# Gate rows for a mixture-of-experts product: from a matrix product on TensorE to DMA reads of a scratch in DRAM

## The reference, cut to what matters

```
xt = layernorm(x)                                  # 1024 tokens x 128
gates = sigmoid(xt @ expert_sel.T)                 # 1024 x 32 experts
gate_full = only the four largest gates of a token kept, the others 0
scores = relu(einsum('nd,edf->nef', xt, keys))     # 32 experts, 64 values each
scores = scores * gate_full[:, :, None]
out = einsum('nef,efv->nv', scores, values)
x = x + tanh(g_ffn) * out
```

## Time and profile before

| | |
|---|---|
| median of 3 runs | 144.35 us (143.78 to 144.61) |
| the profiled execution | 143.71 us |
| its span, first to last instruction | 141.9 us |
| mean granted TensorE clock | 0.984 of full speed |
| PE busy | 130.3 us (92%) |
| DVE busy | 105.3 us (74%) |
| ACT busy | 72.2 us (51%) |
| POOL busy | 9.0 us (6%) |
| DMA packets | 2170, 4.27 MB |

### The profile page before, as it was taken

The page is one execution under the profiler, slowest core; times in us unless marked ns, Lnnn a source line. Parts: engine busy times, 40 slices in busy tenths (PEclk is TensorE's granted clock), DMA queues, the critical chain, the costliest instruction groups (busy, mean ns, idle before and its releaser), DMA issues.

```text
span 141.9 us, 2125 instructions
## 1 busy us (share of the span) xinstructions
PE 130.3 (92%) x672; PEld 86.3 (61%) x672; DVE 105.3 (74%) x338; ACT 72.2 (51%) x172; POOL 9.0 (6%) x27
## 2 busy tenths in 40 slices
PE   5999696998889997999899999999999999999990
PEld 5958393585445864878556346366545666676860
DVE  1799969597989785986989643945694689769852
ACT  5368675587682763336234451331214666866620
POOL 7970000000000000000000000000000000000000
PEclk9999999599999999999999999999999999999998
DMA  4697000000000000000000000000000000000004
GB/s 92 206 387 330 9 5 0 2 0 0 0 5 0 0 0 2 5 0 0 0 0 0 5 0 0 0 2 0 0 0 0 0 0 0 7 0 0 0 0 148
DMA packets 2170, 4.27 MB, mean 30 GB/s; under 512 B 240, under 2 KB 1648, under 8 KB 1904
## 3 DMA queue, kind: packets, MB, share of 16 engines
q1 hardware_dynamic: 2160, 4.15, 8.5%
HBM read 3.63 MB, written 0.52 MB: 29 GB/s over the span
## 4 chain that ended last, share of the span: by engine, by line
PE 77%; DMA 7%; DVE 5%; issue 3%; SPq 3%; ACT 2%; DVEq 0%; ACTq 0%
PE bank L907 11%; PE bank L727 11%; PE bank L831 9%; PE bank L729 9%; PE bank L728 8%; PE bank L897 7%; DMA values<-values_in 7%; PE bank L762 3%; PE bank L841 3%; PE bank L785 2%; PE bank L758 2%; PE bank L736 2%; PE bank L772 2%; PE bank L814 2%; PE bank L816 1%
## 5 line engine op out<-in xcount | busy, mean ns | idle before, releaser
L541 DVE SCALAR_TENSOR_TENSOR keys<-bank,inT 128x512 f32<-128x512 f32 x32 | 22.0, 689 | 12.3 <-PE bank L729 11.3
L695 ACT ACTIVATE inT<-bank 128x512 f32<-128x512 f32 x32 | 18.5, 595 | 22.8 <-PE bank L897 22.7
L907 PE MATMUL bank<-keys,values 128*128 128x512 f32 x32 | 16.6, 614 | 0.0
L727 PE MATMUL bank<-xm_hi,k_lo 128*128 128x512 f32 x32 | 15.4, 480 | 0.0
L736 PE MATMUL bank<-ident 128*128 128x128 f32 x96 | 13.6, 297 | 1.5 <-POOL ident L303 1.5
L831 PE MATMUL bank<-prob,proj 128*65 128x256 f32 x64 | 15.0, 382 | 0.0
L736 PEld LDWEIGHTS bank<-ident 128*128 128x128 f32 x96 | 12.9, 212 | 1.8 <-POOL ident L303 1.5
L729 PE MATMUL bank<-xm_hi,k_hi 128*128 128x512 f32 x32 | 12.6, 395 | 0.0
L728 PE MATMUL bank<-xm_lo,k_hi 128*128 128x512 f32 x32 | 12.6, 394 | 0.0
L442 DVE CUSTOM_DVE_ANT_0 junk<-bank,mask_b 128x512 bf16<-128x512 f32 x16 | 10.4, 689 | 3.0 <-PE bank L785 3.0
L897 PE MATMUL bank<-gateT,expand 64*128 64x512 f32 x32 | 11.9, 496 | 0.0
(11 more groups left out here) (133 smaller groups left out, 244.7 us busy)
## 6 DMA issues: line engine op xcount, KB each, us to landing
keys<-keys_in SPq DMA_DIRECT2D x1, 1024.0 KB, 8.1
values<-values_in SPq DMA_DIRECT2D x1, 1024.0 KB, 10.1
out<-x_mid SPq DMA_DIRECT2D x4, 128.0 KB, 1.9
wa<-wa_in SPq DMA_DIRECT2D x1, 320.0 KB, 3.5
vecs_x<-x_in SPq DMA_DIRECT2D x1, 256.0 KB, 5.7
cx<-ctx_in SPq DMA_DIRECT2D x2, 96.0 KB, 2.7
cx<-ctx_in SPq DMA_DIRECT2D x1, 192.0 KB, 5.8
wb<-wb_in SPq DMA_DIRECT2D x1, 145.0 KB, 6.1
```

The lines of the kernel that those rows point to most:

```text
L541: dve.scalar_tensor_tensor(hid[:, n % 3, :], bank[H_BANK[n % 2]][:, :], 0.0, gated[:, n % 4, :], ALU.max, ALU.mult).then_inc(hid_ready, 1)
L695: act.activation(gated[:, n % 4, :], gates_bank(n)[:, :], ACT.Copy).then_inc(gated_ready, 1)
L727: pe.matmul(o, ll, rh, start=start, stop=False)
L907: last = pe.matmul(bank[ACC_BANK[h]][:, :], values[:, cc], hid[:, n % 3, :], start=(c == 0), stop=(c == EC - 1))
```

## The change

The gates are no longer spread by PE. `select` writes them once (32 experts), `turn_gates` turns them on PE to 32 partitions and ACT copies them. SP then stores them to a scratch in DRAM, `gate_rows` (32 rows of 1024 tokens), one transfer for each batch, and reads them back, one transfer for each chunk: two rows of 512 tokens, each repeated 64 times, onto 128 partitions. The slots of `gated` are now six. `expand`, `one_of`, `spread`, `gates` and DVE's `turn_gates` are gone. The `up` products take turns over three PSUM banks instead of two. All three orders are new. In the PE order `finish 0` stands ahead of the last four `down`.

```diff
-PAIRS = EC // 2
+SLOTS = 6
@@ PE_ORDER (its parts around the gates, and its end)
-    turn_mid 1, out_proj 2, weights 3.1, select 1, turn_gates 0, attend 3.0, turn_gates 1, attend 3.1,
-    spread 0.0, up 0.0, up 0.1, spread 0.1, out_proj 3, spread 0.2, up 0.2, up 0.3, spread 0.3, down 0.0,
...
+    attend 2.1, up 0.0, select 1, weights 3.1, turn_gates 0, out_proj 2, turn_gates 1, attend 3.0, attend 3.1,
+    up 0.1, turn_mid 2, up 0.2, out_proj 3, select 2, up 0.3, up 0.4, down 0.0, down 0.1, up 0.5, down 0.2,
...
+    up 0.11, select 3, up 0.12, down 0.8, down 0.9, turn_gates 2, down 0.10, turn_gates 3, up 0.13, up 0.14,
+    down 0.11, down 0.12, up 0.15, down 0.13, up 1.0, up 1.1, down 0.14, down 0.15, up 1.2, up 1.3, up 1.4,
...
-    down 1.13, down 1.14, down 1.15, finish 0, finish 1
+    finish 0, down 1.12, down 1.13, down 1.14, down 1.15, finish 1
@@ arrays
-        expand = sb("expand", [P, PAIRS * P], F32R)
-        one_of = sb("one_of", [P, 2 * PAIRS])
-        inT = sb("inT", [P, 2, B, S])
+        inT = sb("inT", [P, SLOTS // 2, B, S])
-        gateT = sb("gateT", [P, B, S], F32R)
+        gate = sb("gate", [P, NT, E])
+        gateT = sb("gateT", [E, B, S])
+        gate_rows = nc.dram_tensor("gate_rows", (E, B * S), F32, kind="Internal").ap()
+        gated = inT[:, :, :, :].rearrange("p i b s -> p (i b s)").rearrange("p (i n) -> p i n", i=SLOTS)
-        H_BANK, ACC_BANK = (0, 1), (3, 7)
+        H_BANK, ACC_BANK = (0, 1, 2), (3, 7)
@@ SP, between the loads and the stores of the result
+            for h in range(HALF):
+                for b in range(HB * h, HB * h + HB):
+                    sp.wait_ge(gateT_ready, b + 1)
+                    sp.dma_start(gate_rows[:, S * b:S * b + S], gateT[:, b, :]).then_inc(rows_out[h], 16)
+                sp.wait_ge(rows_out[h], 16 * HB)
+                for c in range(EC):
+                    n = EC * h + c
+                    if n == 0:
+                        sp.wait_ge(proj_done, 3 * B)
+                    if n >= SLOTS:
+                        sp.wait_ge(hid_ready, n - SLOTS + 1)
+                    sp.dma_start(gated[:, n % SLOTS, :],
+                                 gate_rows[2 * c:2 * c + 2, HN * h:HN * (h + 1)].unsqueeze(1).to_broadcast([2, F, HN])).then_inc(gated_in[n % SLOTS], 16)
@@ DVE
-                wide = [P, 4, E]
-                for i, j in enumerate(tiles):
-                    last = dve.scalar_tensor_tensor(gate[:, b % 2, i, :, :], left[:, j, 0:E].unsqueeze(1).to_broadcast(wide), TAKEN,
-                                                    sig[:, j, :].unsqueeze(1).to_broadcast(wide), ALU.is_lt, ALU.mult)
-                last.then_inc(gates_ready, 1)
+                dve.scalar_tensor_tensor(gate[:, t, :], left[:, t, 0:E], TAKEN, sig[:, t, :],
+                                         ALU.is_lt, ALU.mult).then_inc(gates_ready, 1)
-            def turn_gates(b):
...
-                dve.wait_ge(gated_ready, n + 1)
+                dve.wait_ge(gated_in[n % SLOTS], 16 * (n // SLOTS + 1))
@@ ACT
-            def build_expand():
...
-                act.activation(gateT[:, b, :], bank_of(b, TURN_GATES)[:, 0:S], ACT.Copy).then_inc(gateT_ready, 1)
-            def gates(h, c):
...
+                act.activation(gateT[:, b, :], bank_of(b, TURN_GATES)[0:E, 0:S], ACT.Copy).then_inc(gateT_ready, 1)
@@ PE
-                if n < 2:
+                if n == 0:
                     pe.wait_ge(logit_ready, 1)
-                    pe.wait_ge(gate_lo_ready, 2)
-                else:
-                    pe.wait_ge(hid_ready, n - 1)
+                elif n == 1:
+                    pe.wait_ge(gateT_ready, 1)
+                elif n == 2:
+                    pe.wait_ge(logit_ready, 2)
+                if n >= len(H_BANK):
+                    pe.wait_ge(hid_ready, n - len(H_BANK) + 1)
-            def spread(h, i):
...
```

More of the change, by code:

```diff
@@ L58 @@
 PE_ORDER = """
[L59 to L63, removed]
@@ L69 @@
[L69 to L73, removed]
@@ new lines @@
+    attend 0.1, turn_qk 3, row_max 2, weights 1.1, out_proj 0, turn_max 2, row_max 3, attend 1.0, turn_max 3,
+    attend 1.1, weights 2.0, out_proj 1, turn_mid 0, weights 2.1, weights 3.0, attend 2.0, select 0, turn_mid 1,
+    attend 2.1, up 0.0, select 1, weights 3.1, turn_gates 0, out_proj 2, turn_gates 1, attend 3.0, attend 3.1,
+    up 0.1, turn_mid 2, up 0.2, out_proj 3, select 2, up 0.3, up 0.4, down 0.0, down 0.1, up 0.5, down 0.2,
+    up 0.6, up 0.7, down 0.3, down 0.4, up 0.8, turn_mid 3, down 0.5, up 0.9, down 0.6, up 0.10, down 0.7,
@@ L76 @@
 """
 DVE_ORDER = """
[L78 to L87, removed]
@@ new lines @@
+    low_keys 3, low_keys 4, scale_wo 0, norm_qk 3, turn_qk 2, low_keys 5, row_max 2, turn_qk 3, low_values 2,
+    row_max 3, out_proj 0, stats_mid 0, turn_max 2, turn_max 3, norm_mid 0, low_keys 6, out_proj 1, stats_mid 1,
+    low_keys 7, turn_mid 0, norm_mid 1, turn_mid 1, select 0, select 1, out_proj 2, stats_mid 2, low_values 3,
+    norm_mid 2, turn_mid 2, up 0.0, up 0.1, up 0.2, out_proj 3, up 0.3, up 0.4, low_values 4, stats_mid 3,
+    up 0.5, norm_mid 3, up 0.6, select 2, up 0.7, up 0.8, up 0.9, turn_mid 3, low_values 5, low_values 6,
@@ L91 @@
+    up 0.10, select 3, up 0.11, up 0.12, up 0.13, up 0.14, up 0.15, low_values 7, up 1.0, up 1.1, split 1.0,
+    up 1.2, up 1.3, split 1.1, split 1.2, up 1.4, up 1.5, split 1.3, split 1.4, up 1.6, up 1.7, split 1.5,
+    up 1.8, split 1.6, split 1.7, up 1.9, up 1.10, split 1.8, up 1.11, split 1.9, split 1.10, up 1.12, up 1.13,
+    split 1.11, split 1.12, split 1.13, up 1.14, up 1.15, split 1.14, split 1.15, finish 0, finish 1
 """
 ACT_ORDER = """
-    stats_in 0, turn_in 0, stats_in 1, project 0, stats_in 2, turn_in 1, sum_qk 0, split_values 0, project 1,
@@ L94 @@
[L94 to L103, removed]
@@ L104 @@
-    split 1.8, gates 1.12, split 1.9, split 1.10, gates 1.13, finish 0, split 1.11, gates 1.14, split 1.12,
-    gates 1.15, split 1.13, split 1.14, split 1.15, finish 1
+    stats_in 0, turn_in 0, stats_in 1, project 0, stats_in 2, turn_in 1, sum_qk 0, split_values 0, stats_in 3,
+    project 1, turn_qk 0, sum_qk 1, split_values 1, turn_in 2, split_keys 0, project 2, turn_qk 1, weights 0.0,
+    turn_in 3, sum_qk 2, split_keys 1, weights 0.1, project 3, sum_qk 3, split_keys 2, turn_qk 2, turn_qk 3,
@@ new lines @@
+    weights 1.0, attend 0.0, attend 0.1, split_values 2, weights 1.1, split_keys 3, attend 1.0, stats_mid 0,
+    attend 1.1, weights 2.0, turn_mid 0, weights 2.1, stats_mid 1, turn_mid 1, select 0, weights 3.0, attend 2.0,
+    attend 2.1, select 1, weights 3.1, turn_gates 0, turn_gates 1, split_values 3, stats_mid 2, attend 3.0,
+    attend 3.1, turn_mid 2, stats_mid 3, select 2, turn_mid 3, select 3, turn_gates 2, turn_gates 3, split 1.0,
+    split 1.1, split 1.2, split 1.3, finish 0, split 1.4, split 1.5, split 1.6, split 1.7, split 1.8, split 1.9,
@@ L106 @@
+    split 1.10, split 1.11, split 1.12, split 1.13, split 1.14, split 1.15, finish 1
 """
@@ L257, in gated_block @@
         xm_hi_ready, exp_ready, gateT_ready = sem("xm_hi_ready"), sem("exp_ready"), sem("gateT_ready")
-        gated_ready, yT_ready = sem("gated_ready"), sem("yT_ready")
+        yT_ready = sem("yT_ready")
+        rows_out = [sem(f"rows_out{h}") for h in range(HALF)]
+        gated_in = [sem(f"gated_in{i}") for i in range(SLOTS)]
         inT_done, proj_done, qkT_done = sem("inT_done"), sem("proj_done"), sem("qkT_done")
@@ L620, in project @@
                     act.activation(dst, src, ACT.Copy).then_inc(proj_ready, 1)
-            def build_expand():
-                act.wait_ge(one_of_ready, 5)
-                act.activation(expand[:, :].rearrange("p (e f) -> p e f", f=F), one_of[:, :].unsqueeze(2).to_broadcast([P, 2 * PAIRS, F]),
-                               ACT.Copy).then_inc(expand_ready, 1)
             def split_keys(q):
@@ L714, in _ @@
                    "turn_mid": turn_mid, "select": select, "turn_gates": turn_gates,
-                   "build_expand": lambda at: build_expand(), "gates": lambda at: gates(*at), "finish": finish}
+                   "finish": finish}
             for stage, at in stages(ACT_ORDER):
@@ L877, in up @@
                     pe.wait_ge(xm_lo_ready, HB * (h + 1))
-                if n < 2:
+                if n == 0:
                     pe.wait_ge(logit_ready, 1)
-                    pe.wait_ge(gate_lo_ready, 2)
-                else:
-                    pe.wait_ge(hid_ready, n - 1)
-                product(bank[H_BANK[n % 2]][:, :], (k_hi[:, cc], k_lo[:, cc]), (half(xm_hi, h), half(xm_lo, h)),
-                        True, True).then_inc(up_done, 1)
-            def spread(h, i):
-                c = i if h == 0 else 2 * i
-                n = EC * h + c
-                if n == 0:
-                    pe.wait_ge(expand_ready, 1)
-                if i == 0:
-                    pe.wait_ge(gate_lo_ready, 2 * HB * (h + 1))
-                if n >= 1:
```

(10 more changed lines are left out.)

56 lines of the change are left out of this document (16 added, 40 removed).

## The result

The changed kernel takes 250.26 us (median, 249.93 to 256.52) against 144.06 us for the kernel before beside it: a ratio of 1.737, with a 95% interval of 1.726 to 1.747. The prediction of 261 us in a range of 236 to 293 holds it. The profiled execution took 250.03 us and its span is 248.2 us.

The account below looks back on a forecast made before the run. PE bounded the kernel before; two-engine reads would bound the expert layer after. First read lands at 78.6, 31 spacings of 5.5 us, border 2.5, then 3.1 + 4.0 + 1.0: span 259.7, forecast 261 us, range 236 to 293.

Parts of the forecast that it names:

- Two engines: Expert-layer reads: each runs on two DMA engines, 64 rows each, 5.5 us spacing; with overlapping reads 0.80 chance.
- The price of a row: Gate reads: a 2-KB row costs an engine 86.5 ns, linear between 8-KB and 1-KB rows; 5.5 us a read.
- The fixed parts: Around the reads: batch 1 gates at 69.6 us, stored by 71.6, first read's fixed 1.5 us, landing at 78.6.
- six reads under way: Expert-layer reads: six slots let six reads be under way, so 5.5 us is the spacing of chunks.
- The border: Between the halves: SP's queue runs empty once, costing 0 to 4 us, taken as 2.5 us.
- what follows the last product's start: Behind the last read: 3.1 us to the last `down`, 4.0 us to the end, 1.0 us for the lower clock.
- The gates of half 1: At the border: `turn_gates 3` stands behind `down 0.10`, five reads ahead, so these gates are there in time.
- The 24 gate products: PE in the expert layer: 16 singles and 8 pairs removed at 0.62 us each, 14.9 us, all on the path.
- the first rival: Expert-layer reads: sixteen engines carry each read, 0.7 us, hidden under PE; 129 us (124 to 134), chance 0.16.
- the signs foretold: Page after: DMA at 1, about 48 GB/s, 2 small packets a read, landing far above 6 us, PE near 30%.

Follow-up runs that it names:

- the ladder of 2, 4, 8 and 16: Changed kernel (source count 2) against versions storing gate rows 2, 4 or 8 times (source counts 4, 8, 16): 169.82, 137.95 and 135.99 us.
- one row a transfer: Changed kernel with each read split into two transfers of one gate row, each onto 64 partitions: 128.82 us, again 129.02 us.
- the version with six reads: One gate row a transfer, but only the first six chunks read, later ones taking what stands in their slot: 130.43 us.
- POOL's queue: Changed kernel with its 32 reads issued from POOL's queue instead of SP's: 154.19 us, ratio 1.081 to the kernel before.
- two banks: One gate row a transfer, with two PSUM banks for the up products instead of three: 135.21 us; the same in the changed kernel: 251.58 us.
- the old orders: One gate row a transfer with the three orders of the kernel before, less the struck stages: 134.05 us.

## Why the prediction was right, step by step

**Two engines: right, and shown.** The forecast hung on one choice. The count of small packets shows it (2 for each read), the ladder of 2, 4, 8 and 16 shows that the source's outermost count sets it, and the reads of one row show that neither the issue nor the place in DRAM sets the 5.12 us. This agrees with the rule of the Trainium skill that the prediction named (DMA: Bandwidth & Descriptors, section Why a DMA increments its semaphore by 16 and not by 1): k = 2, 4, 8 and 16 were all seen here.

**The price of a row: 80 ns instead of 86.5.** This is the term that was mis-sized (49 + 261/7 is 86.3, either way 5.5 us a read). It was drawn linearly between 8-KB rows read and 1-KB rows stored; the 2-KB rows cost nearly what the 8-KB rows cost by the byte (25.6 against 26.4 GB/s). 31 spacings of 5.12 instead of 5.5 us are 158.9 instead of 170.5 us, 11.6 us less.

**The fixed parts.** The gates of batch 1 were there at 69.3 us instead of 69.6, and their store landed at 70.8 instead of 71.6. The first product with gates started at 78.5, where the read was to land at 78.6, but that agreement is luck: the first read took 7.7 us from its issue (70.79) to the product, of which 5.1 are its rows by the measured price, so its fixed part is 2.6 us and not 1.5, and this made up for the early store and the cheaper rows. Nor were six reads under way, as the prediction took it: SP's fourth issue returned only at 80.2 us (last section). The pace did not depend on it. The border cost 2.1 instead of 2.5 us; what follows the last product's start took 8.8 us, where 8.1 behind the landing were summed, with the clock at 0.50 as foreseen. All in all 78.5 + 158.9 + 2.1 + 8.8 = 248.3, the span; forecast was 259.7, and the price of a row (11.6 us less) accounts for the 11.5 us between, while the fixed parts miss by 0.7 us at most and cancel.

**The gates of half 1** were in time: SP's store of them came at 139.94 us, but the last gates were in SBUF at 134.3. The store landed behind the queued reads, at 155.6 us, and the first read of half 1 had its product 7.0 us after its issue at 155.64: 5.1 us of rows and a fixed part of 1.8, which is most of the border's 2.1 us.

**The 24 gate products, 14.9 us.** In the changed kernel they can't be seen. In the version with one row a transfer the time is 129.0 us: the figure of the first rival, 129, built on them. PE's own work bears the term out: at like clocks (0.987 and 0.984) it is busy 115.6 us in the version with six reads and 130.3 before, 14.7 us less. But the gain in time needs more: new orders are worth 5 us and the third bank 6 us in that version, so 15 us is not what striking the products gives by itself; it is what it gives when PE is kept from waiting. No run struck the products alone.

**What was wrong in the signs foretold:** PE is busy 47% in half 1 (35.3 of 75 us), not near 30%: 1.40 us in 5.12 would be 27%, but at the granted clock of 0.61 its work takes longer; and the page gives no landing time for the reads.

**Left open:** why two, four and, in half 0, eight engines move 25.6 GB/s each, but eight in half 1 and sixteen with one row a transfer only 19.

## What to carry to other kernels

Read a transfer's access patterns from the outside: on SP's queue the outermost count of the source decided the number of DMA engines here, not the 128 partitions of the destination, and a repeated pair of rows ran on two of the sixteen. Count the small packets in the page, one for each engine and transfer on SP's queue: it is the quickest proof. On POOL's queue it was 16 for each read, so there the count proves nothing. Where a step goes off PE through a long latency, its gain is kept only if the orders and the PSUM banks cover the first wait (5 and 6 us here). A wait that is left may be paid again in the clock: it fell to 0.50 behind PE's wait of 2.06 us with two banks, and stayed at 1.00 behind the 1.42 us with the old orders.

## What the runs showed of the hardware that was not expected

- SP is held by its own reads. The chain of the changed kernel at the first reads (start, length):

```profile
70.79 0.63 SPq L293
71.47 0.49 SPq L293
72.00 3.19 SPq L293
75.23 5.00 SPq L293
```

After two quick issues the third takes 3.2 us and the fourth 5.0, as long as a read, though six slots were free: the queue took only a few reads ahead. With one row a transfer (sixteen engines) the first 32 issues took 21.2 us, waits included, and one issue 0.60 us in the median.

- Eight engines took 80 ns for a row of 2 KB in half 0 and 107 ns in half 1 of the same execution, both with all eight busy; two and four took 80 ns in both halves.
- POOL's queue: 0.79 us of POOL for a read of 128 rows, 528 packets, 9.6 us to landing.
- The clock in the attention varies from one execution to the next. The version with one row a transfer had issued its first gate store at 66.3 us in one profile and at 71.9 us in the other, with a granted clock of 1.00 and 0.90 over the first 66 us; from there both took 58.5 us. So the attention makes the whole difference between these two executions (124.8 and 130.4 us of span).
